# GNN layer on one core: PE runs the first layer, the second layer and the segment sums of three successive groups in each step

## The reference

```python
edge_in = concatenate([h[src], h[dst], dist], axis=1)      # 53125 x 129
e = silu(edge_in @ eW1 + eb1)                              # first layer, 128 wide
e = silu(e @ eW2 + eb2)                                    # second layer
agg = segment_sum(e, src, num_segments=3125)
out = silu(concatenate([h, agg], axis=1) @ nW1 + nb1) @ nW2 + nb2
return layernorm(x + out)
```

## Time and profile before

| | |
|---|---|
| median of the runs | 824.6 us |
| the profiled execution: its time, its span | 828.37 us, 826.5 us |
| PE busy | 629.4 us, 76% of the span |
| DVE busy | 481.6 us, 58% |
| ACT busy | 319.7 us, 39% |
| POOL busy | 449.1 us, 54% |
| mean granted PE clock | 0.87 |
| first and last silu1 start | 81.3 us, 807.6 us |
| gathers (POOL, line 618) | 440 of 944 ns in the median, 46.9 to 783.6 us |

### The profile page before, as it was taken

The page is one execution under the profiler, slowest core; times in us unless marked ns, Lnnn a source line. Parts: engine busy times, 40 slices in busy tenths (PEclk is TensorE's granted clock), DMA queues, the critical chain, the costliest instruction groups (busy, mean ns, idle before and its releaser), DMA issues.

```text
span 826.5 us, 15563 instructions
## 1 busy us (share of the span) xinstructions
PE 629.4 (76%) x4815; PEld 501.9 (61%) x4815; DVE 481.6 (58%) x1582; ACT 319.7 (39%) x707; POOL 449.1 (54%) x459
## 2 busy tenths in 40 slices
PE   6874758789778877988398857878786778667796
PEld 3452546667666666666376745657565667556685
DVE  6883767979448755688368845776552233112155
ACT  6422232334433344334143423434343444334365
POOL 1056453547656565574567466665666566556600
PEclk9877867869979896899699969997998899799898
DMA  4111110101111111111111111111111111134201
GB/s 126 45 32 45 27 38 23 30 26 44 42 42 40 39 43 39 39 43 33 42 41 43 34 45 46 42 44 40 45 43 45 39 42 44 40 44 46 45 5 40
DMA packets 17077, 34.15 MB, mean 41 GB/s; under 512 B 8118, under 2 KB 9335, under 8 KB 17000
## 3 DMA queue, kind: packets, MB, share of 16 engines
q0 software_dynamic: 14080, 28.86, 14.4%
q1 hardware_dynamic: 2478, 3.36, 1.5%
q10 hardware_dynamic: 442, 0.93, 0.4%
HBM read 30.67 MB, written 2.40 MB: 40 GB/s over the span
## 4 chain that ended last, share of the span: by engine, by line
PE 55%; another core or an unknown queue 14%; DVE 13%; issue 12%; ACT 4%; DMA 1%; DVEq 1%; ACTq 0%
PE e_ps L626 20%; PE pre_ps L626 13%; PE seg_ps L626 11%; PE sort_ps L626 9%; DVE load_hot L1061 3%; PE turn_ps L730 2%; ACT e L516 2%; ACT hot L496 1%; ACT h L510 1%; DVE col_hot L1056 1%; DVE count L926 1%; DVE agg L1122 1%; DVE row_hot L1057 1%; DMA x_sb<-in_x_dram 1%
## 5 line engine op out<-in xcount | busy, mean ns | idle before, releaser
L618 POOL DMA_INDIRECT q_rows<-q_table,q_index x440 | 445.5, 1012 | 334.2 <-issue 107.3
L1122 DVE TENSOR_TENSOR agg<-agg,seg_ps 128x125 f32 x416 | 93.5, 281 | 251.3 <-PE seg_ps L626 140.1
L626 PE MATMUL seg_ps<-hot,e 128*128 128x125 f32 x880 | 136.2, 302 | 50.6 <-ACT e L516 27.1
L626 PE MATMUL pre_ps<-ident_f,q_rows 128*128 128x128 f32 x440 | 135.5, 308 | 34.0 <-issue 29.8
L626 PEld LDWEIGHTS seg_ps<-hot,e 128*128 128x128 f32 x880 | 118.3, 209 | 58.6 <-ACT e L516 32.2
L626 PE MATMUL pre_ps<-hotT,p_table 128*128 128x128 bf16 x1320 | 151.8, 238 | 0.0
L626 PE MATMUL e_ps<-w_sb,h 128*128 128x128 f32 x880 | 146.3, 317 | 0.0
L510 ACT ACTIVATE h<-pre_ps,eb_sb 128x512 f32<-128x512 f32 x110 | 75.5, 687 | 175.5 <-remote 116.6
L516 ACT ACTIVATE e<-e_ps 128x512 f32<-128x512 f32 x110 | 65.6, 597 | 194.2 <-PE e_ps L626 115.9
L626 PEld LDWEIGHTS e_ps<-w_sb,h 128*128 128x128 f32 x880 | 123.3, 217 | 28.2 <-issue 28.2
L626 PEld LDWEIGHTS pre_ps<-hotT,p_table 128*128 x1320 | 126.6, 109 | 11.0 <-issue 0.6
(11 more groups left out here) (184 smaller groups left out, 504.5 us busy)
## 6 DMA issues: line engine op xcount, KB each, us to landing
q_rows<-q_table,q_index POOLq DMA_INDIRECT x440
q_table<-q_in_sb SPq DMA_DIRECT2D x1, 784.0 KB
x_sb<-in_x_dram ACTq DMA_DIRECT2D x1, 700.0 KB
q_table<-q_in_sb SPq DMA_DIRECT2D x1, 616.0 KB
out_dram<-x_sb SPq DMA_DIRECT2D x1, 364.0 KB
out_dram<-x_sb SPq DMA_DIRECT2D x1, 224.0 KB
w_in<-in_edge_weight_dram SPq DMA_DIRECT2D x1, 185.9 KB
dst_i<-in_dst_dram SPq DMA_DIRECT2D x1, 185.9 KB
```

The source lines that it names most:

```text
L618: P.indirect_dma_start(q_rows[:, g % RING, j, :], None, q_table, bass.IndirectOffsetOnAxis(ap=q_index[:, GT * g + j:GT * g + j + 1], axis= ...
L626: return nc.tensor.matmul(o, lhsT, rhs, start=start, stop=stop, **kw)
L1122: D.tensor_tensor(o, o, seg_ps[:, j * LO:(j + 1) * LO], ALU.add).then_inc(agg_added, 1)
```

## The change

The order inside a step is changed on three engines for the steps up to `TIGHT` = `FLUSH_GROUP` = 103, by one constant:

- PE: `first_layer(m)`, `turn(m+1)`, `second_layer(m-1)`, `segment(m-2)`, the planned parts. In step 103 it does `second_layer(102)`, `segment(101)`, `segment(102)`, the parts and `second_layer(103)`; after that the order is first layer, turn, segment (m-1), parts, second layer (m).
- ACT: `silu2(m-1)` moves from ahead of `silu1(m)` to behind `turned(m+1)`, up to step 103; behind it stand `convert(m)` and `place_weights(m+2)`, as before.
- DVE: `add_segments(m-3)` takes the place of `add_segments(m-2)`; step 103 does both 100 and 101.

No instruction is added or removed, and no buffer is changed. POOL's and SP's lists stay as they are.

```diff
--- before.py
+++ after.py
@@ -150,6 +150,9 @@
 
 
 FLUSH_GROUP = FLUSH // GT
+
+
+TIGHT = FLUSH_GROUP
 SPANS = [(max(0, GT * n - FLUSH % GT), GT * n + GT - FLUSH % GT) for n in range(TILES // GT - FLUSH_GROUP)]
 assert SPANS[-1][1] == WIN
 
@@ -554,7 +557,7 @@
             turned(0)
             place_weights(1)
             for m in range(GROUPS):
-                if m >= 1:
+                if m > TIGHT:
                     silu2(m - 1)
                 for name, k, i in VECTOR.get(m - 1, ()):
                     if name == READ:
@@ -562,6 +565,8 @@
                 silu1(m)
                 if m + 1 < GROUPS:
                     turned(m + 1)
+                if 1 <= m <= TIGHT:
+                    silu2(m - 1)
                 convert(m)
                 if m + 2 < GROUPS:
                     place_weights(m + 2)
@@ -831,16 +836,21 @@
             turn(0)
             for m in range(GROUPS):
                 first_layer(m)
-                if m >= 1:
-                    segment(m - 1)
                 if m + 1 < GROUPS:
                     turn(m + 1)
+                if 1 <= m <= TIGHT:
+                    second_layer(m - 1)
+                if 2 <= m <= TIGHT:
+                    segment(m - 2)
+                if m >= TIGHT:
+                    segment(m - 1)
                 for name, k, i in TENSOR.get(m, ()):
                     if name != CARRY:
                         part(name, k, i)
                 if m == GROUPS - 1:
                     pe.wait_ge(y_read, 1)
-                second_layer(m)
+                if m >= TIGHT:
+                    second_layer(m)
                 n = m - FLUSH_GROUP - 2
                 if n == 1:
                     hidden(0)
@@ -1191,7 +1201,9 @@
             for m in range(GROUPS):
                 if m + 2 < GROUPS:
                     one_hots(m + 2)
-                if m >= 2:
+                if 3 <= m <= TIGHT:
+                    add_segments(m - 3)
+                if m >= TIGHT:
                     add_segments(m - 2)
                 for name, k, i in VECTOR.get(m, ()):
                     part(name, k, i)
```

## The result

The change made the kernel slower: 840.2 us in the median of four runs (836.98 to 842.63) against 826.7 for the kernel before, run beside it. The ratio is 1.016, with a 95% interval of 1.009 to 1.024. The forecast was faster, 804 us, with a range of 768 to 846. The profiled execution after took 837.9 us, for a span of 836.1.

The account below looks back on a forecast made before the run. It took POOL's gathers holding back PE's signals, 6.01 us a step, as the bound. From 828.4, terms -17, -4, -8, +6, +1.5 gave 806.9 us, or 803 against the median; forecast 804, range 768 to 846.

Parts of the forecast that it names:

- rival 1: Late groups: early first layers let POOL run on, e_ready sticks, PE idles and restarts slower; +35, 863 us; chance 0.32.
- The lock: Loop step as a ring of signal, 0.24, four gathers, 1.08, signal: costs 6.01 us whatever PE does inside.
- PE's waits for the silus would vanish: Sign to look for: PE's waits for silu1 and silu2, 51.6 us, all but vanish up to step 103.
- rival 3: Loop: signals mostly in time, POOL at its own pace, some 5.25 us a group; 765 or 762 us; chance 0.15.
- Waits taken off PE: Steps up to 102: half of POOL's waiting beyond the lock is won, -17 us early stretch, -4 late.
- Signals that arrive before the lock closes: Late groups: first layer done early enough that POOL runs eight gathers without a stop; -8 us taken, computed -13.
- the gate: Time in a gather group when PE's signal passes: open at 2.0 us, shut at 3.1; 2.2 expected, nearer to open.
- DVE's later adds: DVE's adds run one group later, making POOL's index about 1.5 us later, four times in the loop: +6 us.
- The seam: Step 103, where PE does segments 101 and 102 together and waits for silu2 and adds: +1.5 us, once.
- The clock: Fewer PE waits should release the clock: some 40 us less in the early stretch, result 764; left out of the sum.

Follow-up runs that it names:

- after_2: The changed kernel once more, unaltered, run beside the kernel before (819.6 us): 829.4 us, ratio 1.011.
- segonly_2: Kernel before with only segments and their adds one group later: 811.5 us, 0.991, with late signals; first run (segonly), chip without late signals, 681.4 us, 1.007.

## Why the prediction was wrong

The forecast was a gain of 21.5 us, and the profiled executions differ by 9.6 us the other way. The measured 840.2 us lies inside the stated range of 768 to 846 only because rival 1 had stretched it that far.

**The lock** was read rightly. It is in the trace after at 6.08 us a step, and without gathers it is gone. So is the reading that PE's waits for the silus would vanish (51.6 us to 1.6) and give little. The chip without late signals also shows rival 3's price: with POOL at its own pace the kernel before takes 676 us. I had applied it to parts of the loop only.

**Waits taken off PE**, -17 early and -4 late: up to step 36 the change gained 10.6 us of the 17 (15.5 in after_2, of which up to some 9 can come from the set). The late part without boundaries, 72 to 103, gained 1.8 (after_2: 6.2). The early term was too large by about 6 us, the late one by about 2.

**Signals that arrive before the lock closes**, -8: this is the step that failed, in size and in sign: in place of -8 the parts 36 to 72 gave +20.8 us. I let the first layer end 2.4 us after the signal, 2.2 us after POOL's start, where the gate is still open. In the steady step it does begin 1.27 us after silu1, but takes 1.94 us in place of 1.2, so that it ends 2.98 us after POOL's start, and the gate is shut. There it gains nothing. I had taken the 1.2 us from a step in which the first layer stood behind the second. A part of the 1.94 us is the clock, 0.76 of full speed from 740.7 to 742.7; but in after_2 the first layer from 743.65 to 745.42 takes 1.77 us at a clock of 1.00, so there is another cause, and no run shows it. In front of the boundaries, behind the long gather, signals do come early, POOL does run four groups in a row, and that is no gain, because the chunk ends there and the index isn't ready. The second and longer wait for the index then becomes a second stream, behind which `e_ready` is held. I had priced this chain as rival 1, with the right links (a stuck `e_ready`, ACT at silu2, PE idle, then half clock) and at half weight with 842 us, close to the measured 840.2. That agreement is luck: I took it for a matter of every third group, and it happens at the boundaries of chunks, three times. The parts 36 to 72 cost 7.13 us a step after (256.8 / 36), 6.56 before; rival 1 had 6.83 against 6.32.

**DVE's later adds**, +6: POOL's waits for the index grew by 47.2 - 31.8 = 15.4 us in the loop. The smaller part of it is my reason. Counted from silu1 of the steps 42, 54 and 66, POOL gets its index after 2.98, 2.92 and 2.41 us before and after 3.97, 4.69 and 4.63 us in the changed kernel: 5.0 us later in all, close to the 6. With the segments alone moved (segonly_2, where they still stand right behind the first layer) it is 2.92, 3.11 and 1.50 us. The larger part, some 10 us, I left out: the index is late for a POOL that comes early.

**The seam**, +1.5: silu1 of step 103 to the end took 48.0 us against 47.0, and 48.5 in after_2. Right. Without gathers it would be larger: 48.6 against 45.2 us.

**The clock.** The prediction weighed what the Trainium skill (TensorE: Matmul & The Clock Gate, Part 1) says, that activity releases the clock, and the 764 us that would follow. The early stretch agrees in direction: fewer waits, 0.85 instead of 0.81. The late one went the other way, 0.91 to 0.87, and the whole fall lies in the stretch with the boundaries. From 350 to 600 us, first before and then after (columns of the earlier trace rows):

```profile
350.00:600.00 250.00, 192.67 (x1602) 153.95 (x1600) 165.93 (x528) 95.30 (x206) 155.28 (x153) 0.91 0.15 41
350.00:600.00 250.00, 191.68 (x1480) 150.28 (x1478) 152.47 (x494) 85.58 (x190) 145.75 (x140) 0.84 0.14 38
```

From 600 to 780 us it is 0.91 in both. This fits the new idle time at the boundaries, behind which the clock stood at 0.50 for 12 us; no run tests it apart. Taking waits off one engine isn't the same as keeping it busy.

**What is open.** The streams at steps 38, 50 and 62 of the changed kernel begin with a gather that a scan of DVE seems to stretch; that the scan is the cause is not tested. Between them, the second layer of m-1 and the moved silu2 bring it about at all three boundaries (segonly_2 has it at none), and no run separates the two. Nor do they show by what path a gather delays another engine's signal, or whether PE itself is held as well: in the second stream, from 388.90 to 392.57, its segment matmuls stand still for 0.36 to 0.94 us between each other, and the profile names nothing that they wait for.

## What to carry to other kernels

When an engine's completion and its semaphore are far apart in a trace, find what another engine does in that time before reordering anything; here a kernel without the gathers told it in one look. A queue that may run far ahead is no gain if it ends at a wait: the stream in which it catches up holds others. Ask where an earlier start will stand next, and try the one-line limit on the run-ahead before an order of three engines; but measure it where the kernel will run, since on the one chip without late signals the limit, with its short rest, was a loss of 2.4%.

## What the runs showed of the hardware

- While POOL issues indirect DMAs back to back, a completion of PE can become visible late: the first layer's signal 2.87 us after its last matmul, and, across the rest of a stream of twelve gathers and the group of four behind it, a second layer's 16.7 us, against 0.03 us without gathers. This was so in five of the six sets of runs, those in which the kernel before took 820 to 827 us.
- A gather that began 0.06 us after a 1.56 us scan on DVE took 2.25 us in place of 0.94 (after, 350.17; the same at 436.89 and 525.65).
- One chip, in the one set that ran on it, did not delay signals. With the same gathers (0.94 us, 0.30 between) PE's signals came in 0.03 us, and the kernel before took 676.4 us instead of about 820, 18% less. A difference between two chips can be larger than anything that a change of order brings, and a verdict holds for its kind: segonly was 0.7% slower there and 0.9% faster on a chip with late signals.
- A memset of 0.14 us between two gathers fits into the 0.30 us that POOL leaves between them and cost nothing that showed on a chip with late signals (784.7 us, two runs, against 788.4 without it).
